# A two-lane decoder kernel: weights prepared later, the second lane begun at once, row maxima sent in blocks of eight heads

## The chip, the cores and the metric

One core of one Trainium2 chip runs the whole program. The metric is the device time of one execution in microseconds, the median of several runs. Smaller is better.

## The reference

Two decoder layers in float32 on x of shape (4, 256, 128). Layer 0 is self-attention of 16 heads of 8 columns with a learned relative bias that is added after the softmax, cross-attention to a context (16 heads of 64, a padding mask and a causal mask), and a feed-forward part whose activations and weights are quantized, with a depthwise convolution and SiLU. Layer 1 is causal self-attention with linear biases, a second attention over the heads of each token, and a mixture of eight experts with two chosen. Each part reads the layer norm of x and adds to x.

```
attn = softmax(einsum('bhqd,bhkd->bhqk', q, k) * scale)        # layer 0, first part
out  = einsum('bhqk,bhkd->bhqd', attn + rel_bias, v)           # 16 heads, 256 keys
...
scale = 1 / clip(mean(abs(w)), 1e-5); wq = clip(round(w*scale), -1, 1) / scale
```

The quantized weights need the mean absolute value of each weight matrix, and cross-attention needs, for rows whose keys are all closed, the product Wv Wo; both are found once, on the chip, before they are used.

## The kernel before

The batches are shared out to two lanes, A (batches 0 and 1) and B (batches 2 and 3). Each lane has its own half of the free on-chip memory, four of the eight PSUM banks, and its own program of six stages: `rel_attention` (tiles named l0a), `cross_attention` (l0x), `quantized_ffn`, `alibi_attention` (l1a), `head_attention` (l1x) and `expert_ffn` (moe). Each engine has one queue and works in its order. That order is written out by hand as text in `TURNS` (L2389 on): "A4 W1 A5" means four steps of lane A, one of the weight program W, five of lane A. A step is what a stage's program does between two `yield`s. The times behind `yield` order the parts within a stage; between the lanes only `TURNS` counts. Nothing is reordered at run time: a step that waits for a semaphore holds all behind it on its engine. L in SyncE's turns is the loading of weights that reuse the place of earlier ones: first the weights of l1x (when both lanes have left l0a), then the experts' (when both have left l0x).

**W**, `weight_levels` (L2129), loads most weights, converts constants to bfloat16, and prepares the quantized weights and the product Wv Wo: a sum of absolute values (DVE, L2174), a matmul with ones (L2198), five DVE operations to the levels (L2179 to L2192), eight transposes of Wv (L2201), two copies by ACT (L2213), sixteen matmul records for the product (L2206) and a scaled copy (L2217). Its buffers lie at the start of lane B's memory and it writes to lane B's banks 0 to 3. So lane B's first stage waits for it (`ready(..., "arena")`, L2259, on the semaphore `levels`), and in `TURNS` lane B's first TensorE step stands behind 32 steps of lane A.

**The first stage, l0a.** It normalizes x, transposes it (L172) and the context (L639), and for each of four token tiles projects q, k and v (L653), splits q and k into bfloat16 parts (DVE L572 and L575; POOL L493 and L496), stacks them (POOL L502, ACT L537), transposes the stacks (L668) and copies them out to `qkT` (DVE L465, ACT L517). Before that POOL clears the buffers (L483 to L488).

**The attention loop** is the class `Attention`, used by l0a and l1a. A softmax without overflow needs each row's maximum before the exponentials. So every head is multiplied twice: `tensor_S` makes the scores row by row and `vector_max` (L330) takes the negated maxima. When all 16 heads of a batch are done, `vector_parts` (L332) splits the maxima into three bfloat16 parts by four or five small chained DVE operations, `tensor_shift` (L238) transposes them, `vector_shiftT` (L356) copies them, and `sync_shift` (L251) sends them by DMA into three spare rows of the query tile. `tensor_E` then makes the transposed scores with the maxima already taken off, ACT exponentiates (L364), and `tensor_PV` multiplies with the values (L292). A score job is one head in l0a and one to four heads in l1a (`self.jobs`): 16 jobs a batch in l0a, 12 in l1a. Batch 0's jobs all run before the loop, in l0a as pairs of heads whose 64-row matmuls alternate between the two halves of the array (`tensor_S_pair`, L296, two PSUM banks); batch 1's are spread over the first twelve heads of the loop (`ahead`, one bank, L226). After the first shift TensorE also runs eight matmuls whose result nobody reads (L248). In l0a, a fourth of the stack copies are ACT's (`by_scalar`, L428).

## Time and profile before

| | us |
|---|---|
| median of 3 runs | 611.25 |
| lowest and highest | 607.7, 611.59 |
| the profiled execution's own time | 614.77 |
| its span, first to last instruction | 613.0 |
| TensorE busy in it | 533.3 |
| DVE busy | 420.4 |
| mean granted TensorE clock | 0.948 |

The span is cut into stretches to read it: a stretch where TensorE is busy nearly all the time at a granted clock of 1.00 can't be shortened without taking matmuls away; a stretch where it idles, or where its clock is granted at half (0.50 in the profile: 1.2 instead of 2.4 GHz), holds the time that an order of work can win or lose. The mean clock of a stretch lies between the two.

### The profile page before, as it was taken

How to read it: one execution, taken by the hardware profiler on the slowest of the kernel's cores; microseconds unless marked ns; L12 is line 12 of the kernel's file. 1: busy time of each engine (PE TensorE's matmuls, PEld its weight loads, DVE VectorE, ACT ScalarE, POOL GpSimd, SP SyncE). 2: the span in 40 equal slices, each digit the busy share in tenths (PEclk: the TensorE clock that was granted, in tenths of full speed). 3: DMA queues.
4: the chain of work that ended last, by engine and by line, in shares of the span. 5: the costliest groups of instructions: out<-in, count | busy, mean ns of one | idle time of the engine just before them, and what ended most of it. 6: DMA issues, size and time to landing. Idle time of an engine off the chain costs nothing.

```text
span 613.0 us, 12971 instructions
## 1 busy us (share of the span) xinstructions
PE 533.3 (87%) x4858; PEld 328.1 (54%) x4858; DVE 420.4 (69%) x1229; ACT 328.5 (54%) x809; POOL 193.8 (32%) x288
## 2 busy tenths in 40 slices
PE   4767797998999989877995679988998989999995
PEld 2433344344555656556453556666666866755554
DVE  5784664574454774898769876757548677589796
ACT  2413444457767785597644346544675548364341
POOL 5553300042235454332621031001023221434765
PEclk9966889999999999889997799999999999999998
DMA  8700000000002000000237105210000000402101
GB/s 290 280 1 3 2 3 3 2 3 2 2 18 120 2 1 2 2 1 1 66 111 267 26 12 163 79 31 2 4 3 2 2 2 3 139 0 80 59 2 34
DMA packets 25816, 27.92 MB, mean 46 GB/s; under 512 B 18177, under 2 KB 22794, under 8 KB 24858
## 3 DMA queue, kind: packets, MB, share of 16 engines
q1 hardware_dynamic: 25754, 27.10, 13.3%
q8 instruction: 39, 0.64, 0.4%
q14 instruction: 23, 0.19, 0.1%
HBM read 22.14 MB, written 4.75 MB: 44 GB/s over the span
## 4 chain that ended last, share of the span: by engine, by line
PE 66%; DVE 17%; ACT 5%; issue 4%; DMA 2%; POOL 2%; SPq 2%; POOLq 0%; DVEq 0%; ACTq 0%
PE B_banks L2086 5%; PE A_banks L292 4%; PE A_banks L2086 4%; PE B_banks L292 3%; DVE A_l0a_nmax L330 3%; PE A_banks L1011 2%; PE A_banks L998 2%; PE B_banks L1852 1%; PE B_banks L2118 1%; PE B_banks L998 1%; PE A_banks L951 1%; PE A_banks L1852 1%; PE A_banks L953 1%; PE B_banks L953 1%; PE B_banks L1862 1%
## 5 line engine op out<-in xcount | busy, mean ns | idle before, releaser
L818 POOL TENSOR_TENSOR A_l0x_prob<-A_l0x_prob,A_l0x_inverted_sums 128x256 f32<-128x256 f32 (+1 forms) x32 | 25.9, 829 | 54.1 <-DVE A_l0x_inverted_sums L932 54.0
L818 POOL TENSOR_TENSOR B_l0x_prob<-B_l0x_prob,B_l0x_inverted_sums 128x256 f32<-128x256 f32 (+1 forms) x32 | 27.1, 866 | 41.1 <-DVE B_l0x_inverted_sums L932 41.1
L2086 PE MATMUL A_banks<-A_moe_xT,w_moe_rows 128*128 128x512 f32 x72 | 35.1, 600 | 0.0
L330 DVE TENSOR_REDUCE B_l0a_nmax<-B_banks 128x2 f32<-128x512 f32 x32 | 21.5, 688 | 19.3 <-PE B_banks L226 13.6
L2086 PE MATMUL B_banks<-B_moe_xT,w_moe_rows 128*128 128x512 f32 x72 | 34.5, 596 | 0.0
L364 ACT ACTIVATE A_l0a_expT<-A_banks 128x512 f32<-128x512 f32 x32 | 18.3, 598 | 26.9 <-PE A_banks L316 26.9
L835 ACT ACTIVATE B_l0x_prob<-B_l0x_prob,B_l0x_nmax 128x128 f32<-128x128 f32 x64 | 28.3, 444 | 6.2 <-DVE B_l0x_nmax L914 6.2
L330 DVE TENSOR_REDUCE A_l0a_nmax<-A_banks 128x2 f32<-128x512 f32 x32 | 21.4, 689 | 13.8 <-PE A_banks L226 12.0
L835 ACT ACTIVATE A_l0x_prob<-A_l0x_prob,A_l0x_nmax 128x128 f32<-128x128 f32 x64 | 28.2, 446 | 2.2 <-DVE A_l0x_nmax L914 2.2
L364 ACT ACTIVATE B_l0a_expT<-B_banks 128x512 f32<-128x512 f32 x32 | 18.6, 599 | 11.6 <-PE B_banks L316 11.5
L998 PE MATMUL B_banks<-w_const_rows,B_l0x_prob 128*128 128x128 f32 x96 | 17.4, 292 | 7.9 <-ACT B_l0x_probT L852 5.0
L914 DVE CUSTOM_DVE_ANT_0 A_l0x_prob<-A_banks,A_l0x_mask_q 128x128 f32<-128x128 f32 x64 | 19.0, 353 | 7.2 <-PE A_banks L986 6.0
L1982 ACT ACTIVATE B_moe_h<-B_banks,w_moe_rest_rows 128x512 f32<-128x512 f32 x18 | 12.3, 684 | 20.3 <-PE B_banks L2086 20.3
L1715 POOL TENSOR_TENSOR A_l1x_prob<-A_l1x_prob,A_l1x_rz 128x512 f32<-128x512 f32 x8 | 8.3, 1042 | 46.2 <-DVE A_l1x_rz L1796 46.2
L852 ACT ACTIVATE B_l0x_probT<-B_banks 128x384 f32<-128x384 f32 x32 | 15.5, 484 | 13.5 <-PE B_banks L998 13.5
L364 ACT ACTIVATE A_l1a_expT<-A_banks 128x384 f32<-128x384 f32 x32 | 14.9, 494 | 13.9 <-PE A_banks L272 13.9
L364 ACT ACTIVATE B_l1a_expT<-B_banks 128x384 f32<-128x384 f32 x32 | 15.3, 494 | 11.7 <-PE B_banks L272 11.5
L852 ACT ACTIVATE A_l0x_probT<-A_banks 128x384 f32<-128x384 f32 x32 | 15.6, 488 | 11.0 <-PE A_banks L998 11.0
L330 DVE TENSOR_REDUCE B_l1a_nmax<-B_banks 128x2 f32<-128x512 f32 (+1 forms) x24 | 16.1, 686 | 6.1 <-PE B_banks L234 6.0
L914 DVE CUSTOM_DVE_ANT_0 B_l0x_prob<-B_banks,B_l0x_mask_q 128x128 f32<-128x128 f32 x64 | 18.9, 349 | 1.1 <-PE B_banks L986 0.9
L998 PEld LDWEIGHTS B_banks<-w_const_rows,B_l0x_prob 128*128 128x128 f32 x96 | 10.9, 146 | 15.9 <-issue 8.8
L2086 PEld LDWEIGHTS A_banks<-A_moe_xT,w_moe_rows 128*128 128x128 f32 x72 | 12.7, 190 | 11.9 <-issue 10.8
(612 smaller groups left out, 1574.5 us busy)
## 6 DMA issues: line engine op xcount, KB each, us to landing
w_toeplitz_rows<-in_toeplitz_rows SPq DMA_DIRECT2D x1, 3072.0 KB, 15.7
w_moe_rows<-in_moe_rows SPq DMA_DIRECT2D x1, 2304.0 KB, 8.6
w_l1x_rows<-in_l1x_rows SPq DMA_DIRECT2D x1, 2048.0 KB, 8.6
A_l1x_values<-A_l1a_v_tokens SPq DMA_DIRECT2D x4, 512.0 KB, 2.6
A_l1x_v_groups<-A_l1x_values SPq DMA_DIRECT2D x16, 128.0 KB, 3.2
B_l1x_values<-B_l1a_v_tokens SPq DMA_DIRECT2D x4, 512.0 KB, 3.2
B_l1x_v_groups<-B_l1x_values SPq DMA_DIRECT2D x16, 128.0 KB, 3.2
w_l0x_vo_rows<-in_l0x_vo_rows SPq DMA_DIRECT2D x1, 1024.0 KB, 8.8
```

The costliest lines, as they stand in the source:

```text
L292: ins = pe.matmul(bank[r:r + self.rows, second:S], lhsT, rhs, start=(part == 0), stop=(part == parts - 1), skip_group_check=True)
L330: dve.tensor_reduce(out, scores, AX, ALU.max, negate=True).then_inc(self.s_mx.sem, 1)
L364: act.activation(self.expT[:, u % self.ring, :], self.exp_bank(u)[:, 0:self.W], ACT.Exp, scale=self.scale).then_inc(self.s_p.sem, 1)
L818: ins = pool.tensor_tensor(pair, pair, bcast(rz[:, g % 2, i, :], 2, n), ALU.mult)
L835: ins = act.activation(part, part, ACT.Exp, bias=nmax[:, b, i, h:h + 1], scale=-1.0, accum_out=zsum[:, g % 2, i, u % 2:u % 2 + 1])
L852: act.activation(probT[:, u % 4, :], bank[2][:, 0:W], ACT.Copy).then_inc(s_pt.sem, 1)
L914: ins = dve.tensor_tensor_reduce(prob[:, (2 * p + j) % RING, at:at + n], bank[j][:, at:at + n], mask_q[:, b, at:at + n], 1.0, 3e38, ALU.ad ...
L953: ins = pe.matmul(bank[n % 3][:, :], w["l0x_k"][:, c * P:(c + 1) * P], cT[:], start=True, stop=True)
L998: ins = pe.transpose(bank[2][:, c * P:(c + 1) * P], prob[:, u % RING, c * P:(c + 1) * P], w["ident"][:])
L1011: ins = pe.matmul(bank[3][HD * j:HD * (j + 1), part * P:S], vals[:, b * SB + part, h * HD:(h + 1) * HD], pT[:, S:W] if part else pT[:, 0:S ...
L1982: act.activation(h1[:, n % 2, :], hidden_bank(2 * n)[:, :], ACT.Identity, bias=w["moe_b1"][:, e, part:part + 1]).then_inc(s_h1.sem, 1)
L2086: pe.matmul(hidden_bank(k)[:, :], w["moe_w3" if which else "moe_w1"][:, ORDER[i], part, :], xT[:], start=True, stop=True).then_inc(s_h.sem, 1)
```

## The change

Four edits come together.

1. `weight_levels` becomes part of lane A's side: its buffers lie at the end of lane A's memory, its matmuls use lane A's bank 0 only, in four rounds (sum, four transposes, four transposes, product), and it waits until lane A has copied out its last shift (`bank_left`). Its turns stand in the middle of lane A's attention loop. The uses of `levels` wait in l0x instead of in lane B's l0a. The loads of the table `toeplitz` and of the l0x weights go ahead of its raw weights.
2. Lane B begins with the others: its first TensorE turn stands behind 4 steps of lane A. Each lane's POOL clears its buffers before the norm, and the context is transposed after x (bank 3).
3. The maxima go in blocks of `HB` = 8 heads, four blocks a stage instead of two; 12 heads' jobs (`AHEAD`) run before the loop and the others are spread over the whole loop. The first shift stands between job 8 and job 9. The paired form of the score jobs and the eight matmuls without a reader go. Stack copies of the last two tiles are all ACT's.
4. All of `TURNS` is new. SyncE's second late load stands behind one SyncE step of lane A's l1a instead of behind six.

```diff
-EARLY = 4
+HB = 8
+AHEAD = 12
...
+    def due(self, n):
+        return min(self.BLOCKS * self.JOBS, -(-(n + 1 + AHEAD) * self.JOBS // HB))
+    def completed(self, n):
+        k = self.due(n) // self.JOBS
+        return k - 1 if n >= 0 and k * self.JOBS > self.due(n - 1) else None
     def score_bank(self, m):
-        return self.bank[m % 2 if m < self.JOBS else 0]
+        return self.bank[m % 2 if m < self.JOBS else (m + 1) % 2 if m < self.first else 0]
...
-        if b == 0:
-            for _ in range(8):
-                pe.matmul(self.bank[2][:, :], self.w["ident_bf"][:], self.w["other_token"][:]..., start=True, ...)
+        self.shifted = k
...
-    by_scalar = [n % 4 == 3 for n in range(STEPS)]
+    by_scalar = [n % 4 == 3 or n >= 4 * SB for n in range(STEPS)]
...
     def gpsimd(pool):                                  # l0a
-        yield 2.0
+        yield 0.0
+        pool.memset(vals[:], 0.0).then_inc(s_init.sem, 1)
         pool.memset(stack[:, :, 0, :, 6 * HD:SW], 0.0)
...
-        for u in range(a.JOBS):                        # l0a and l1a, on TensorE
+        for u in range(a.first):
-            if u % 2 == 0:
-                a.tensor_S_pair(pe, u)
+            if u == a.JOBS:
+                a.tensor_shift(pe, 0)
+            a.tensor_S(pe, u)
...
         for n in range(U + 8):
-            if h == H - EARLY and b + 1 < NB:
-                a.tensor_shift(pe, b + 1)
+            k = a.completed(n - 1)
+            if k is not None:
+                a.tensor_shift(pe, k)
...
+    st.at = lane.end - 3 * P * 4 - (2 * HID * 2 + HP * P + 16) * 4       # weight_levels(lanes[0], ...)
-        for group in ("const_16", "l0a", "B_x"):
+        for group in ("const_16", "l0a", "B_x", "toeplitz", "padding", "l0x_vo", "l0x"):
     def tensor(pe):
-        yield 9.5
+        yield 60.0
+        pe.wait_ge(*lane.bank_left)
         pe.wait_ge(*s_part(1))
         pe.matmul(bank[0][:, 0:2], w["ones"][:], part[:], ...).then_inc(s_sum.sem, 1)
+        for i in range(2):
+            pe.wait_ge(*(s_vT(1) if i else s_mean(1)))
+            for c in range(4):
+                ins = pe.transpose(bank[0][:, c * P:(c + 1) * P], w["l0x_v"][:, ...], w["ident"][:])
+        pe.wait_ge(*s_vT(2))
...
 TURNS = {
     "tensor":
-        "A4 W1 A5 W1 A23 B1 A3 B1 A3 B2 A4 B2 ...
+        "A4 B2 A2 B2 A5 B2 A3 B3 A4 B2 A1 B3 A10 B3 ... A1 B1 A2 W2 B2 A1 B1 W1 A2 B1 W1 ...
     "gpsimd":
-        "A15 B2 A1 B14 A11 ...
+        "A2 B1 A1 B1 A3 B1 A3 B3 A2 B2 ...
     "sync":
-        "W2 A1 W11 B1 A2 B2 L1 A6 L1 A3 B5 ...
+        "W1 A1 W1 B1 W11 A1 B1 A1 B1 A2 B2 L1 A1 L1 A7 B3 ...
```

## Rows read from the trace of the kernel before

**Rows 1.** The page: its first line and the busy time of each engine.
```profile
span 613.0 us, 12971 instructions
...
PE 533.3 (87%) x4858; PEld 328.1 (54%) x4858; DVE 420.4 (69%) x1229; ACT 328.5 (54%) x809; POOL 193.8 (32%) x288
```

**Rows 2.** Busy time by stretch: us, width, five engines' busy us, PEclk granted clock, DMA.
```profile
0.00:31.00 31.00, 17.62 (x106) 11.37 (x106) 20.09 (x59) 10.51 (x29) 16.61 (x34) 0.98 0.77 282
...
31.00:48.00 17.00, 10.55 (x56) 5.28 (x58) 12.83 (x26) 3.48 (x9) 10.16 (x16) 0.73 0.01 2
...
48.00:99.00 51.00, 42.67 (x408) 20.25 (x407) 31.48 (x76) 23.04 (x54) 8.08 (x19) 0.80 0.01 2
...
99.00:120.00 21.00, 18.89 (x159) 8.27 (x160) 11.53 (x31) 10.14 (x21) 1.02 (x1) 0.92 0.01 2
...
120.00:170.00 50.00, 47.96 (x420) 22.29 (x420) 26.23 (x109) 33.00 (x89) 14.31 (x20) 1.00 0.01 2
...
240.00:290.00 50.00, 41.27 (x336) 30.53 (x335) 41.07 (x151) 32.94 (x95) 16.79 (x23) 0.93 0.01 1
...
290.00:340.00 50.00, 39.77 (x269) 23.80 (x268) 39.10 (x119) 26.47 (x76) 15.78 (x43) 0.90 0.46 144
...
340.00:360.00 20.00, 14.59 (x123) 11.60 (x121) 16.52 (x48) 7.21 (x11) 0.01 (x1) 0.81 0.01 2
```

**Rows 3.** The chain that ended last, two pieces of it: start us, us, what.
```profile
97.10 2.21 DMA B_l0a_qkT<-B_l0a_shiftT
...
167.68 1.86 PE B_banks L292 x32
```

**Rows 4.** Timeline, 4 to 48 us: start us, us, engine, line, operation.
```profile
7.32 1.47 DVE L164 TENSOR_SCALAR A_l0a_xn<-A_x,A_l0a_mv,A_l0a_rstd 128x128 f32<-128x128 f32 x4
...
22.69 0.86 DVE L148 BATCH_NORM_STATS2 B_l0a_bn<-B_x 128x6 f32<-128x128 f32 x4
...
35.67 3.88 DVE L164 TENSOR_SCALAR B_l0a_xn<-B_x,B_l0a_mv,B_l0a_rstd 128x128 f32<-128x128 f32 x4
...
36.21 2.69 POOL L486 MEMSET B_l0a_vals<- 128x3072 f32 x1
...
47.91 0.39 PE L316 MATMUL A_banks<-A_l0a_qkT 64*128 64x256 bf16 x4 [1.83 <-DMA A_l0a_qkT<-A_l0a_shiftT]
```

**Rows 5.** Timeline of TensorE: the score matmuls of lane A and the shift.
```profile
27.95 0.39 PE L302 MATMUL A_banks<-A_l0a_qkT 64*128 64x256 bf16 x4 [1.05 <-DVE A_l0a_nmax L330]
...
44.07 0.28 PE L244 MATMUL A_banks<-w_ident_bf,A_l0a_parts 128*128 128x128 bf16 x2
...
44.19 1.89 PE L248 MATMUL A_banks<-w_other_token,w_ident_bf 128*128 128x512 bf16 x8
...
48.14 0.38 PE L226 MATMUL A_banks<-A_l0a_qkT 64*128 64x256 bf16 x2
```

**Rows 6.** Groups by line, 0 to 110 us: busy us, mean ns of one, idle before.
```profile
L330 DVE TENSOR_REDUCE A_l0a_nmax<-A_banks 128x2 f32<-128x512 f32 x32 | 21.4, 689 | 13.8 <-PE A_banks L226 12.0 <-PE A_banks L302 1.8
...
L502 POOL COPY A_l0a_expT<-A_l0a_split 128x256 bf16<-128x256 bf16 (+1 forms) x16 | 5.6, 393 | 0.3
...
L712 PE MATMUL A_banks<-w_const_rows,A_l0a_xT 128*128 128x128 f32 x16 | 3.4, 297 | 1.3 <-ACT A_l0a_xT L555 1.3
...
L496 POOL TENSOR_TENSOR A_l0a_split<-A_l0a_rest_qk,A_l0a_split 128x256 bf16<-128x256 f32 x4 | 2.7, 669 | 0.3
...
L2206 PE MATMUL B_banks<-w_l0x_vo_rows,B_wq_vT 128*128 128x128 f32 x16 | 2.0, 276 | 0.0
...
L345 DVE CAST A_l0a_parts<-A_l0a_nmax 128x32 bf16<-128x32 f32 x2 | 0.4, 182 | 0.1
```

**Rows 7.** Busy time by a short stretch, columns as in the second group.
```profile
52.00:54.00 2.00, 2.00 (x5) 0.59 (x4) 1.02 (x2) 0.67 (x2) 0.00 (x0) 0.50 0.00 0
```

**Rows 8.** Timeline of lane A's second attention, at its first shift.
```profile
349.85 0.28 PE L244 MATMUL A_banks<-w_ident_bf,A_l1a_parts 128*128 128x128 bf16 x2 [3.65 <-DVE A_l1a_parts L354]
```

**Rows 9.** Timeline of SyncE's queue: the load of the experts' weights.
```profile
322.74 0.57 SPq L2249 DMA_DIRECT2D w_moe_rows<-in_moe_rows  x1
```

More of the change, by code:

```diff
@@ L216, in tensor_S @@
     def tensor_S(self, pe, m):
-        b, at = divmod(m, self.JOBS)
-        c, h, n = self.jobs[at]
+        b, c, h, n = self.job(m)
         bank = self.score_bank(m)
-        if b:
+        if m == self.JOBS or m >= self.first:
             pe.wait_ge(*self.s_mx(m))
@@ L364, in scalar_exp @@
         act.activation(self.expT[:, u % self.ring, :], self.exp_bank(u)[:, 0:self.W], ACT.Exp, scale=self.scale).then_inc(self.s_p.sem, 1)
-def ahead(n, jobs):
-    b, h = divmod(n, H)
-    if b + 1 >= NB:
-        return range(0)
-    done, now = (min(jobs, k * jobs // (H - EARLY)) for k in (h, h + 1))
-    return range(jobs * (b + 1) + done, jobs * (b + 1) + now)
 def split_columns(part_of):
@@ L677, in tensor @@
                     transpose_stack(n)
-        for u in range(a.JOBS):
+        for u in range(a.first):
             yield SCORES + 1.2 * u - 0.4
@@ L1593, in tensor @@
             ins.then_inc(s_stT.sem, 1)
-        for u in range(a.JOBS):
+        for u in range(a.first):
             yield SCORES + 3.0 + 0.75 * u - 0.4
@@ L2155, in sync @@
             sp.dma_start(raw[:, i, :], raw_dram[i]).then_inc(s_raw.sem, 16)
-        for group in ("l0x_vo", "toeplitz", "padding", "l0x", "l1a", "ffn", "l1x_rest", "moe_rest"):
+        for group in ("l1a", "ffn", "l1x_rest", "moe_rest"):
             yield
@@ L2160, in vector @@
     def vector(dve):
-        link = Chain(dve, lane)
+        link = Chain(dve, st)
         yield 3.9
```

284 lines of the change are left out of this document (144 added, 140 removed), and 46 rows, old and new, of the table TURNS.

## Prediction

> **What bounds the kernel now.** I read the page first: TensorE is busy 533 of 613 us [rows 1], so it is the bound on the average, and what an order can win is the rest: 80 us of idle time, and time at half clock. Then the table of busy time by stretch shows where these lie [rows 2]. I multiply TensorE's busy time by the mean granted clock, which gives its work in us at full clock (an estimate, since a mean is used): 0 to 31 us: 17.62 x 0.98 = 17.3. 31 to 48: 10.55 x 0.73 = 7.7. 48 to 99: 42.67 x 0.80 = 34.1. 99 to 120: 18.89 x 0.92 = 17.4. 120 to 170: 48.0. So the first 120 us do only 76.5 us of work and leave 43.5, while from 120 on TensorE is nearly full at clock 1.00, a rate of 0.96. The second hole is 240 to 360: 120 - 41.27 - 39.77 - 14.59 = 24.4 us idle, with clocks of 0.93, 0.90 and 0.81.
>
> Third, why the start is empty. Lane B's norm runs at 22.69, its normalized x is written only at 35.67 [rows 4], its first exponential scores come after the DMA of 97.10, and its last product of values is at 167.68 [rows 3]. Lane A's first exponential scores are at 47.91 and had waited 1.83 us for the shift's DMA [rows 4]. Until 48 the rate is 25.0/48 = 0.52, with lane A going from TensorE to DVE and back alone: a pair of score jobs, then 1.05 us of waiting for the maxima [rows 5].
>
> **Part 1, lane B at once.** Total work to the state that before has at 170: 17.3 + 7.7 + 34.1 + 17.4 + 48.0 = 124.5 us. The change alters it so. A pair of heads takes 0.39 us for four matmuls, a single job 0.38 for two [rows 5]: before, a lane has 8 pairs and 16 singles, 3.1 + 6.1 = 9.2; after, 32 singles, 12.2. That is +3.0 a lane, +6.0. Two more shifts a lane at 0.28 [rows 5]: +1.1. The eight matmuls without a reader go, 1.89 a lane [rows 5]: -3.8. W's matmuls move, they aren't added. Sum 127.8.
>
> When do both loops begin? By 48 TensorE has done 25.0; without W (about 4; its product alone is 2.0 [rows 6]), the readerless 1.9 and some 3 of lane B, lane A's preparation is some 16, and with 12 single jobs (4.6) for 8 pairs (3.1) it is 17.6. Two lanes: 35, of which I put 33 before the loops. POOL bounds the pace: it needs 0.67 + 5.6/4 = 2.1 us a token tile for two of its three steps [rows 6], so eight tiles take at least 17 us, after both lanes' clearing (the longest fill is 2.69 [rows 4]) and norms. DVE has 24 maxima of 0.689 [rows 6], 16.5 us, beside the splits. I take 45 us (bounds 41 and 49: lane A alone needed 48 with 16 maxima before the loop in place of 12, and there is more beside it).
>
> Left are 127.8 - 33 = 95 us of work. The two loops are: per lane eight groups of values at 1.86 [rows 3], 16 pairs of exponential scores at 0.39 [rows 4], 20 jobs at 0.38, transposes 3.4 [rows 6]: 14.9 + 6.2 + 7.6 + 3.4 = 32.1, both 64.2. The other 31 are projections, which before ran at 0.96: 32 us. At what rate two loops run together is the open cost. Its bounds are 34.1/51 = 0.67 (48 to 99, one loop beside a preparation) and 0.96. I take 17.4/21 = 0.83, from 99 to 120, the one stretch in which, for most of it, both loops run [rows 2]. That gives 64.2/0.83 = 77 us. W now lies inside: TensorE waits behind its sum for DVE, and twice for ACT's copies, 0.5 us or so each; I take 2 us (0 to 4). Sum: 45 + 32 + 77 + 2 = 156, against 170: -14 us. With the bounds of the rate: 146 (-24) and 175 (+5).
>
> Clearing buffers is moved too. While POOL filled lane B's values from 36.21 for 2.69 us, DVE's four normalizing operations took 3.88 us; lane A's took 1.47 at 7.32, beside shorter fills [rows 4]. After the change POOL goes from lane A's norm straight to lane B's long fill, so lane A's may take 3.88: +2.4 us (0 to 2.4), inside the 41 to 49.
>
> The Trainium skill says on this (SBUF — State Buffer, "Who interferes with whom") that VectorE in a two-port mode and GpSimd lock each other out for a whole instruction; by it every one of lane A's four could meet a fill. Lane B's row agrees with such a lock and lane A's is milder, and by the page the start would be some 4 us later instead of 2.4.
>
> **Part 2, blocks of eight heads.** In the loop a stage now sends three shifts, not one. Each costs DVE four or five operations near 0.18 [rows 6] and a copy, about 1.1 us; over four stages 8 more, 9 us of DVE, whose busy time is 420 us of 613 [rows 1]. Each is finished four heads before it is needed, so the chain of DVE, TensorE, DVE and DMA (4 x 0.18, 0.28, a copy of about as long, 2.21 [rows 3, 5, 6]: 3.5 us) is covered; without that cover it would cost 3.5 us a block. The first shift is covered by the four jobs after it: that is inside the 45. In l1a lane A's TensorE stood 3.65 us before its first shift [rows 8], in a stretch of clock 0.81 [rows 2]. Nine jobs stand there instead of twelve, and three of them behind the shift. I take -3 us for lane A (bounds -5 and +1, since DVE is busy 16.52 of 20 us there and gets the extra operations), and nothing for lane B, whose l1a runs beside work of lane A.
>
> **Part 3, the rest of the turns.** From 170 on I cost them at +3 (bounds -3 and +8): the lag of lane B behind lane A, in steps, is smaller than before (lane B is at 43 to 61% when lane A is at 50 to 66%, against 37 to 51%), and with less lag both lanes sit in the feed-forward part or in the maxima of l1a together. There the cover, the other lane's projections, is thinner. SyncE now loads the experts' weights after one step of lane A's l1a instead of six [rows 9]; it waits for lane B's end of l0x. As long as that end comes before lane A's l1a it costs nothing.
>
> **Sum.** -14 - 3 + 3 = -14 on the profiled 614.77 us, 600.8. That execution lies 3.5 us above the median of the runs, 611.25, so the forecast is 597.
>
> **Rival 1, the loops overlap fully** (rate 0.96, l1a -5, rest 0): -24 - 5 = -29, 582. For: two lanes always have something else to issue. Against: in 99 to 120 they did not. 0.16.
>
> **Rival 2, the time comes back later.** The start gains 10 to 14, but between 240 and 360 DVE is the limit (41.07, 39.10 and 16.52 busy [rows 2]), the lanes meet there and lose 8, and the second late load holds lane A's DMAs: -4 or so, 607. Or the clearing and POOL's tiles hold lane B so that it doesn't really begin early; the same size. 0.2.
>
> **Rival 3, slower.** The place is the double loop of l0a. TensorE's queue is in order, a score job waits for its lane's DVE maximum, and the other lane's work stands behind it; the gaps let the clock fall. This happened before: at 52 to 54 TensorE was busy all of 2.00 us at clock 0.50 [rows 7], 6 us after the eight readerless matmuls. If the double loop runs like 48 to 99, at 0.67, the 170 becomes 175; with +2.4 for the fills, -1 for l1a and +6 for the lost lag the sum is +12: 623. It decides from a rate of 64.2/(170 - 79) = 0.71 downwards. 0.1.
>
> The Trainium skill (TensorE: Matmul & The Clock Gate, "HAM oscillation — how this bites in real kernels") warns of this too: waits between bursts of matmuls let the engine fall back to half rate. The row at 0.50 agrees. By it, taking the readerless matmuls out would leave the clock lower and the third rival would be likelier.
>
> **Chances and range.** Main case 0.54 (own range 590 to 604), rivals 0.16, 0.2, 0.1. A measurement of this kernel tells about 1%, 6 us, from no change. Faster by over 1% (below 605): 0.54 + 0.16 + a fifth of rival 2 = 0.74; within 1%: 0.15; slower: 0.11. The range 583 to 612 leaves out half of rival 1 and rival 3.
>
> **What would show it.** Right: lane B's first projection near 18 us instead of past 39.5 (35.67 + 3.88); both lanes' first exponential scores between 41 and 49; lane B's last product of values near 150 instead of 168; TensorE's work by clock of 64 us or so in the double loop at a rate near 0.83; no wait of TensorE on a shift's DMA over 0.5 us; lane A's wait before its first shift in l1a below 1 us; W's steps between lane A's last shift and its last exponentials with waits of 2 us together. Wrong: granted clocks below 0.8 between 45 and 110; waits for maxima in the double loop of over 15 us; more idle time of TensorE between 240 and 360 than 24 us; a SyncE queue that stands on the late load while lane A's l1a needs it.

## The result and the profile after

The changed kernel takes 603.0 us (median of 4 runs, 600.85 to 606.53) beside 610.0 for the kernel before on the same chip (4 runs, 607.7 to 611.59): ratio 0.990, 95% interval 0.987 to 0.993. That is 1.0% faster, 7.0 us, where 14 us (2.3%) were forecast. The profiled execution took 606.53 us against 614.77 before, 8.2 us less; each lies at or above the slowest of the four executions of its kernel. Two executions among the runs below, 1653 and 2665 us long, were disturbed and are left out.

The page of the changed kernel, its first line and the busy time of each engine; they answer to [rows 1]:

```profile
span 604.6 us, 13037 instructions
...
PE 522.7 (86%) x4832; PEld 323.9 (54%) x4842; DVE 427.1 (71%) x1261; ACT 330.7 (55%) x819; POOL 191.4 (32%) x288
```

TensorE is busy 10.6 us less and the span is 8.4 us shorter: its idle time did not fall, its busy time did. The busy time by stretch of the changed kernel, in the columns of [rows 2]:

```profile
0.00:31.00 31.00, 15.54 (x104) 9.53 (x104) 21.19 (x59) 12.13 (x36) 24.36 (x49) 1.00 0.78 281
31.00:48.00 17.00, 14.60 (x103) 6.79 (x102) 14.67 (x28) 12.21 (x30) 8.67 (x19) 0.72 0.01 3
48.00:99.00 51.00, 41.47 (x407) 19.19 (x408) 33.05 (x87) 21.45 (x46) 0.00 (x0) 0.79 0.01 2
99.00:120.00 21.00, 20.18 (x239) 10.80 (x239) 11.10 (x39) 12.04 (x27) 0.00 (x0) 1.00 0.01 3
120.00:170.00 50.00, 49.30 (x320) 22.31 (x318) 25.86 (x115) 32.74 (x92) 16.33 (x22) 1.00 0.00 1
240.00:290.00 50.00, 38.04 (x292) 27.36 (x292) 40.94 (x146) 34.15 (x102) 17.32 (x25) 0.91 0.01 1
290.00:340.00 50.00, 39.61 (x263) 24.16 (x260) 41.61 (x125) 23.78 (x56) 14.66 (x47) 0.92 0.47 141
340.00:360.00 20.00, 18.23 (x124) 10.45 (x125) 15.86 (x41) 9.74 (x29) 4.43 (x17) 0.91 0.32 97
```

The reader is to compare three rows. 48 to 99, which was to be the double loop at a rate of 0.83, reads 41.47 us at a clock of 0.79 and stood at 42.67 at 0.80 before: TensorE is no fuller there. 31 to 48 is fuller (14.60 busy for 10.55), but at a clock of 0.72. And 0 to 31 is emptier. Only 99 to 170 is visibly fuller (1.5 us idle for 4.2, clock 1.00 throughout). How full a stretch is doesn't say how far the two lanes have come in it; that is read below.

A finer sum shows it in three parts: over windows of 2 us, idle is the width less TensorE's busy time, work is busy time by granted clock, and loss is the rest of the busy time, what the half clock costs. I use these words below; the sums are good to a few us, no better, for two reasons. Neighbouring records overlap: busy time falls by 10.6 us, but the busy times of all groups of matmul records, added up, by only 6.1. And a trace is one execution: in 240 to 360, where the score jobs of l0a have no part, the kernel before loses 10.0 us to the half clock, and with nothing but l0a's score jobs changed 5.4.

| us | before: idle, work, loss | after: idle, work, loss |
|---|---|---|
| 0 to 48 | 19.8, 24.5, 3.6 | 17.9, 25.7, 4.5 |
| 48 to 100 | 8.7, 34.4, 8.9 | 9.5, 33.5, 9.0 |
| 100 to 170 | 3.8, 64.7, 1.5 | 1.5, 68.5, 0.0 |
| 170 to the end | 47.4, 384.8, 10.8 | 52.9, 369.7, 12.0 |

By 170 us the changed kernel has done 127.7 us of work, just what the forecast said was needed for the state that before has at 170 (127.8). But it had come further than that state. Lane B's last values, its first projection of l0x and a matmul of lane A's l0x, in the changed kernel and then the last two in the kernel before:

```profile
149.31 1.05 PE L312 MATMUL B_banks<-w_toeplitz_rows,B_l0a_vals 128*32 128x256 f32 x16
152.38 1.02 PE L960 MATMUL B_banks<-w_l0x_vo_rows,B_ctxT 128*128 128x512 f32 x2
...
173.51 0.66 PE L982 MATMUL A_banks<-w_l0x_vo,A_l0x_ctx_sum_by_token 128*128 128x128 f32 x4
```

```profile
170.32 1.02 PE L951 MATMUL B_banks<-w_l0x_vo_rows,B_ctxT 128*128 128x512 f32 x2
...
177.28 0.66 PE L973 MATMUL A_banks<-w_l0x_vo,A_l0x_ctx_sum_by_token 128*128 128x128 f32 x4
```

Lane B is 18 to 19 us ahead of its old time (its last values end at 150.4; before, the group at 167.68 [rows 3] ends at 169.5) and lane A 4. From the end of its l0a to 170 lane B does 9.0 us of work that the kernel before does only after 170 (the changed kernel's instructions on lane B's banks alone):

```profile
150.40:170.00 19.60, 9.03 (x18) 1.00 0.00 0
```

Lane A does 1.8 us more in the same way (167.5 to 170). Take these off, and the state that before has at 170 took 117 us of work and was reached near 160. So the start gained some 10 us of the 14 forecast (an estimate, from the busy time on each lane's banks; taken at other states between 164 and 290 us it gives 8 to 11), and behind 170 next to nothing was added to it or lost: the span is 8.4 us shorter.

The start, from the timeline of the changed kernel (start us, us, engine, line, operation; in brackets the idle time before and what ended it):

```profile
6.73 2.66 POOL L482 MEMSET B_l0a_vals<- 128x3072 f32 x1
7.30 4.11 DVE L2179 CAST w_ident_bf<-w_const_rows 128x128 bf16<-128x128 f32 x1 [1.68 <-DMA w_const_rows<-in_const_rows]
7.44 4.04 DVE L2180 CAST w_mask_q<-w_const_rows 128x128 bf16<-128x128 f32 x1
...
12.29 1.10 DVE L165 TENSOR_SCALAR A_l0a_xn<-A_x,A_l0a_mv,A_l0a_rstd 128x128 f32<-128x128 f32 x4
...
12.77 1.16 PE L173 MATMUL A_banks<-w_const_rows,A_l0a_xn 128*128 128x128 f32 x4 [12.77 <-DVE A_l0a_xn L165]
...
17.98 1.61 DVE L165 TENSOR_SCALAR B_l0a_xn<-B_x,B_l0a_mv,B_l0a_rstd 128x128 f32<-128x128 f32 x4
...
20.76 1.53 PE L656 MATMUL B_banks<-w_l0a_rows,B_l0a_xT 128*128 128x384 f32 x4
```

Lane A's normalized x is written at 12.29, not at 7.32 [rows 4]: DVE first waits 1.68 us for the constants, and its first two casts to bfloat16 then stretch over 4 us. POOL clears lane B's buffers beside them, in fills of 2.66, 0.95, 0.79 and 0.38 us that end at 11.33; the casts end at 11.41 and 11.48. TensorE's first instruction of all is at 12.77. Lane B's first projection, 20.76, is near the forecast 18.

The exponential scores (line 327 now) of lane A and the first of lane B, same columns:

```profile
44.06 0.39 PE L327 MATMUL A_banks<-A_l0a_qkT 64*128 64x256 bf16 x1
...
49.00 0.61 PE L327 MATMUL A_banks<-A_l0a_qkT 64*128 64x256 bf16 x4
...
53.38 0.61 PE L327 MATMUL A_banks<-A_l0a_qkT 64*128 64x256 bf16 x4
...
59.73 0.39 PE L327 MATMUL A_banks<-A_l0a_qkT 64*128 64x256 bf16 x4
...
61.81 0.40 PE L327 MATMUL B_banks<-B_l0a_qkT 64*128 64x256 bf16 x4 [0.22 <-DVE B_l0a_nmax L340]
```

Lane A's first, at 44.06, lies in the 41 to 49 that was forecast for both; lane B's first is at 61.81. Lane A's pairs come 4 to 6 us apart. Four matmuls take 0.61 us there and 0.39 outside: that is the half clock. The two stretches around it, in the columns of [rows 2]:

```profile
44.00:62.00 18.00, 14.22 (x104) 5.92 (x104) 11.77 (x27) 7.11 (x14) 0.00 (x0) 0.58 0.01 2
62.00:80.00 18.00, 14.57 (x132) 6.23 (x132) 10.80 (x29) 6.58 (x13) 0.00 (x0) 0.72 0.01 2
```

In 2 us windows that is 8.0 us of work in the first 18 us and 9.8 in the next, 0.44 and 0.54 of full rate; in the kernel before 9.1 and 11.3. From 80 to 100 the changed kernel does 17.7 in 20, from 100 to 116 15.2 in 16: the double loop is not slow once the clock is full. TensorE's four longest sums of waits in 31 to 120 (what waited, for what: us in total, times, longest):

```profile
PE A_banks L248 <- DVE A_l0a_nmax L340: 4.6, 8, 0.9
PE B_banks L248 <- DVE B_l0a_nmax L340: 2.3, 3, 0.9
PE A_banks L264 <- DVE A_l0a_parts L367: 1.6, 1, 1.6
PE B_banks L248 <- DVE B_l0a_shiftT L373: 1.0, 1, 1.0
```

The idle gaps are short, 1.6 us at the longest, and the half clock around them costs more than they do: 11.0 us of loss against 7.2 of idle time in 44 to 80. No shift's DMA is among the waits, as forecast, and lane B's last values at 149.3 are where the forecast had them (near 150).

### The profile page after: what moved, and what is told of

It is laid out like the page before. It is cut to its first block, busy times and chain, and to the rows that moved or that the text cites. A ratio compares the mean times of both kernels' runs of the same rounds, so it can differ in the third digit from the quotient of the medians.

```text
span 604.6 us, 13037 instructions
## 1 busy us (share of the span) xinstructions
PE 522.7 (86%) x4832; PEld 323.9 (54%) x4842; DVE 427.1 (71%) x1261; ACT 330.7 (55%) x819; POOL 191.4 (32%) x288
## 4 chain that ended last, share of the span: by engine, by line
PE 64%; DVE 19%; ACT 5%; issue 5%; POOL 3%; DMA 2%; SPq 1%; POOLq 0%; DVEq 0%; ACTq 0%; another core or an unknown queue 0%
PE A_banks L312 4%; PE B_banks L312 4%; PE A_banks L2098 3%; PE B_banks L2098 3%; PE A_banks L1020 2%; PE A_banks L1007 2%; DVE A_l0a_nmax L340 2%; PE B_banks L1007 2%; PE B_banks L1823 2%; PE B_banks L1020 2%; PE B_banks L248 1%; PE B_banks L975 1%; PE A_banks L975 1%; PE B_banks L962 1%; PE B_banks L960 1%
## 5 line engine op out<-in xcount | busy, mean ns | idle before, releaser
L379 ACT ACTIVATE A_l0a_expT<-A_banks 128x512 f32<-128x512 f32 x32 | 18.6, 608 | 29.5 <-PE A_banks L327 29.5
L160 POOL TENSOR_TENSOR A_l0a_rstd<-A_l0a_ve,w_const_rows 128x4 f32<-128x4 f32 x2 | 2.0, 1012 | 79.9 <-DVE A_l0a_ve L156 79.9
L379 ACT ACTIVATE B_l0a_expT<-B_banks 128x512 f32<-128x512 f32 x32 | 18.5, 606 | 10.2 <-PE B_banks L327 10.2
L1007 PE MATMUL B_banks<-w_const_rows,B_l0x_prob 128*128 128x128 f32 x96 | 17.7, 295 | 6.4 <-ACT B_l0x_probT L859 4.1
L1994 ACT ACTIVATE A_moe_h<-A_banks,w_moe_rest_rows 128x512 f32<-128x512 f32 x18 | 12.3, 684 | 18.5 <-PE A_banks L2098 18.5
L859 ACT ACTIVATE A_l0x_probT<-A_banks 128x384 f32<-128x384 f32 x32 | 15.5, 484 | 10.9 <-PE A_banks L1007 10.8
L340 DVE TENSOR_REDUCE A_l1a_nmax<-A_banks 128x2 f32<-128x512 f32 (+1 forms) x24 | 16.3, 689 | 5.9 <-PE A_banks L256 5.6
```

The costliest lines, as they stand in the source:

```text
L340: dve.tensor_reduce(out, scores, AX, ALU.max, negate=True).then_inc(self.s_mx.sem, 1)
L379: act.activation(self.expT[:, u % self.ring, :], self.exp_bank(u)[:, 0:self.W], ACT.Exp, scale=self.scale).then_inc(self.s_p.sem, 1)
L859: act.activation(probT[:, u % 4, :], bank[2][:, 0:W], ACT.Copy).then_inc(s_pt.sem, 1)
L1007: ins = pe.transpose(bank[2][:, c * P:(c + 1) * P], prob[:, u % RING, c * P:(c + 1) * P], w["ident"][:])
L1994: act.activation(h1[:, n % 2, :], hidden_bank(2 * n)[:, :], ACT.Identity, bias=w["moe_b1"][:, e, part:part + 1]).then_inc(s_h1.sem, 1)
```

## The experiments

All ran beside the kernel before (609.4 to 611.1 us in these sets). Ratios are to it, with their 95% interval; "against the changed kernel" is the ratio divided by 0.9899. Where the text says by how much the start was reached sooner or later, it is the state of both lanes that before has near 174 us, found as above.

### The matmuls without a reader

In the kernel before (line 245 on) they are taken out:

```diff
-        if b == 0:
-            for _ in range(8):
-                pe.matmul(self.bank[2][:, :], self.w["ident_bf"][:], self.w["other_token"][:]...)
```

> The kernel before with one edit: the eight matmuls without a reader after each first shift (L248) are gone, nothing else. Theory 1 (the change's gain is TensorE work taken away: between the two traces TensorE's idle time went from 79.7 to 81.9 us, its loss to the half clock from 24.9 to 25.5, its work from 508 to 497): removing them alone gives most of the gain, 4 to 7 us against before. Rival (the gain is from lane B's early start, and the readerless matmuls were hidden in the wait for the shift's DMA): 0 to 1.5 us, or slower, since the clock falls earlier.

Measured: 616.6 us, 1.009 [1.0059, 1.0122], 0.9% slower: the theory that the gain is TensorE work taken away fell. In the changed kernel the same eight go back, in l0a in front of the first exponential scores (behind the twelve score jobs), in l1a behind the first shift:

```diff
+    def readerless(self, pe):
+        for _ in range(8):
+            pe.matmul(self.bank[2][:, :], self.w["ident_bf"][:], self.w["other_token"][:]..., ...)
...
         wait_copied(pe, STEPS - 1)                     # l0a
+        a.readerless(pe)
...
             if u == a.JOBS:                            # l1a
                 a.tensor_shift(pe, 0)
+                a.readerless(pe)
```

> The changed kernel with the eight readerless matmuls put back, once per stage, before the first exponential scores in l0a and after the first shift in l1a. Theory 1: the gain over before shrinks from 7 us to 0 to 3 us. Rival (they cost nothing, or they keep the clock up in the double loop of l0a, which ran at a clock of about 0.67 from 48 to 80 us): the same as the changed kernel within 1 us, or faster.

Measured: 605.8 us, 0.9933 [0.9913, 0.9952]. So taking them out costs the kernel before 5.5 us and gives the changed kernel some 2, by the ratios; the second is at the edge of what the intervals tell. Put another way: with them in both kernels the rest of the change is worth 4 us, with them in neither some 12. The stretch 44 to 62, first of the kernel before without them, then of the changed kernel with them (the changed kernel's own stands above):

```profile
44.00:62.00 18.00, 12.72 (x63) 5.81 (x60) 9.74 (x22) 6.91 (x18) 4.52 (x12) 0.59 0.01 2
```

```profile
44.00:62.00 18.00, 14.95 (x102) 6.04 (x100) 10.63 (x25) 6.43 (x13) 0.00 (x0) 0.69 0.01 2
```

With them the clock is 0.69 in the changed kernel, without them 0.58; in the kernel before 0.68 and 0.59. The clock is higher with them in both. The clock is not all of it: without them the kernel before has 7.7 us less work, 9.8 us more idle time and 0.4 us more loss over its span (2.2 more up to 100 us). But before, they fill a wait for a DMA in which there is nothing else; in the changed kernel other work of both lanes stands behind them. That this is why they cost there is the reading that fits; no run varied it by itself. They are 8.4 us of records in all, l1a's as well as l0a's, and the sum had counted only l0a's 3.8.

### Score jobs in pairs or one by one

The changed kernel gets the paired form back for the jobs ahead of the loop:

```diff
-            a.tensor_S(pe, u)
+            if u % 2 == 0:
+                a.tensor_S_pair(pe, u)
```

> The changed kernel with the 12 score jobs before l0a's loop issued as six pairs again (four matmuls on both halves of the array), all else as in the change. The prediction's term: +6 us of TensorE work for both lanes from single jobs, of which 12 of 32 jobs are undone here, so 2 to 2.5 us less work. Theory A (the term was real and on the path): 1.5 to 2.5 us faster. Rival (single jobs of one lane run beside the other lane's on the other half of the array, or DVE's maxima pace this stretch): 0, or slower by up to 2 us, since a pair waits for both maxima before it.

Measured: 609.3 us, 0.9988 [0.9973, 1.0003], 0.9% above the changed kernel. Its stretch 44 to 62:

```profile
44.00:62.00 18.00, 11.42 (x79) 4.98 (x81) 12.41 (x27) 7.00 (x13) 0.00 (x0) 0.50 0.01 2
```

A clock of 0.50 throughout. A pair waits for the maxima of both banks, and the queue stands meanwhile for the other lane too; in 44 to 80 the idle time is 11.0 us for 7.2, and the longest sum of waits is a new one, of lane B's pairs:

```profile
PE B_banks L325 <- DVE B_l0a_nmax L354: 3.9, 3, 1.7
```

The start is reached 5.6 us later. Both expectations had missed: one had it faster, the other slower by 2 us at most. The reverse in the kernel before, with its own turns:

```diff
-            if u % 2 == 0:
-                a.tensor_S_pair(pe, u)
-            else:
+            a.tensor_S(pe, u)
+            if u % 2:
                 yield
                 transpose_stack(4 * SB + u // 2)
```

> The kernel before with its first sixteen score jobs issued one head at a time and each waiting for the maximum that frees its own bank, instead of in pairs that wait for both maxima; the turns are those of before. The reverse test (pairs in the changed kernel) had cost 6 us. Theory (the single jobs help where two lanes share TensorE, and cost more work of it where one lane runs alone; in the kernel before each lane's sixteen first jobs run alone): 0 to 2 us faster, ratio 0.997 to 1.000. Rival (single jobs are worth 6 us wherever they stand, and the early lane B is worth nothing): 0.988 to 0.992. Other rival (the weight loads, which a pair shares out better, cost 3 us more per lane): 1.003 to 1.010.

Measured: 608.2 us, 0.9963 [0.9937, 0.9989]: 2.3 us faster, just past what the theory gave. So a third of the change's 1% is to be had by this edit alone. And the change with pairs kept ahead of l0a's loop is worth nothing that can be measured: in these turns, which were made for single jobs, the early lane B pays only together with them.

### A later fill, and lane B late again

Lane B's POOL waits with its clearing until lane A's normalized x is written, and lane A's norm is let go ahead of it:

```diff
     def gpsimd(pool):
+        w[f"{lane.name}_xn"] = s_xn(TT)
         yield 0.0
+        if lane.name == "B":
+            pool.wait_ge(*w["A_xn"])
```

> The changed kernel with one wait more on POOL: lane B's buffers are cleared only once lane A's normalized x is written. In the changed kernel DVE's two casts of the constants took 4.11 us beside POOL's fill of 2.66 us, and lane A's transposed x came at 12.77 us instead of 7.86. Theory 2 (the start is bound by lane A's chain through DVE, POOL and TensorE): lane A's transposes begin near 8.5 to 9 us and the whole is 2 to 4 us faster than the changed kernel. Rival (POOL's and DVE's total work bounds the start, so lane B loses what lane A wins; or the double loop after it absorbs it): within 1 us of the changed kernel.

Measured: 602.5 us, 0.9884 [0.9862, 0.9907], not told from the changed kernel. The collision is gone, lane A's x is there 4.3 us earlier:

```profile
8.00 1.11 DVE L165 TENSOR_SCALAR A_l0a_xn<-A_x,A_l0a_mv,A_l0a_rstd 128x128 f32<-128x128 f32 x4
...
9.17 2.66 POOL L485 MEMSET B_l0a_vals<- 128x3072 f32 x1 [2.26 <-DVE A_l0a_xn L165]
...
42.79 0.39 PE L327 MATMUL A_banks<-A_l0a_qkT 64*128 64x256 bf16 x1
```

but its first exponential scores come only 1.3 us earlier. The fill is not the cause of the missing gain.

The other way round, `TURNS` with lane B's steps of l0a later, which gives it a third to a half of its old lag back: its first TensorE step stands behind 19 steps of lane A (before 32, changed kernel 4), its 60th behind 96 (before 118, changed kernel 85), the other engines' strings to match.

```diff
 TURNS = {
     "tensor":
-        "A4 B2 A2 B2 A5 B2 A3 B3 A4 B2 A1 B3 A10 B3 ...
+        "A19 B2 A4 B1 A2 B1 A9 B2 A1 B3 A7 B1 A1 B2 ...
```

> The changed kernel with another order: all of lane B's steps of l0a are put 25 us later at the start, fading to none at 170 us; lane A, the weight steps, the blocks of eight heads and everything after 170 us are as in the change. Theory S (lane B's early start is worth something only if the rest of the order uses it; here it does): slower than the changed kernel by 10 us or more, with lane B's stages late by 10 us or more at every later milestone. Rival (lane B's start is worth nothing, since TensorE's total work decides): within 4 us of the changed kernel.

Measured: 632.5 us, 1.038 [1.0357, 1.0408], 4.9% above the changed kernel. Lane A's l0a then ends at 139.6 (changed 124.1, before 119.1), and the start is reached 24 us later. It was the expected direction, 10 us or more. But it is 3.8% slower than the kernel before, which has all of the lag. So the merged order is bad here, and what an early lane B is worth by itself is not shown by this run: these turns were made by a rule and not tuned, and other orders cost as much (below).

### The pace of the maxima

`vector_max` reads fewer keys, so that the shift isn't the reference's; everything else stays. Half of the keys, in either kernel:

```diff
-            out, scores = self.nmax[:, b, :, h], bank[:, :].rearrange("p (c k) -> p c k", c=SB)
+            out, scores = self.nmax[:, b, :, h], bank[:, :].rearrange("p (c k) -> p c k", c=SB)[:, :, 0:P]
```

> The changed kernel with each maximum of l0a taken over the first 128 of the 256 keys only: the reduction reads half as much, so its 0.689 us become some 0.42, and TensorE's work is the same. The shift is then not the row's maximum (that part of the computation is changed). Theory D (from 28 to 110 us both lanes wait for DVE: TensorE to DVE and back is what paces l0a): 64 maxima by 0.27 us are 17 us of DVE, and 5 to 10 us of the whole go. Rival (the half clock and the in-order queue pace it): under 2 us.

> The kernel before with the same edit (maxima of l0a over half the keys). In it lane A's l0a runs alone on DVE until 35 us. Theory D: it gains as well, 3 to 8 us, since 12.0 us of DVE's idle time and 5.1 + 3.9 us of TensorE's lie between score jobs and maxima of lane A. Rival: under 2 us.

> The changed kernel with the maxima of lane-wide score jobs taken over half of the keys, as in an earlier run (0.978 of the kernel before) whose profiled execution was disturbed; sent for a profile. If the maxima hold back lane B's first exponential in the changed kernel, it starts before 56 instead of at 61.8, and idle time plus half-clock loss in 48 to 100 falls from 18.5 to under 13; if the order of turns and the half clock hold it, it starts after 59 and that sum stays over 16. Ratio 0.975 to 0.982.

An eighth of them (`0:32`):

> The changed kernel with these maxima over 32 of the 256 keys (the shift is then not the reference's). Theory (the maxima's round trips between TensorE and VectorE keep TensorE partly idle and thereby at half clock in 48 to 100 us): another 3 to 6 us beyond the half maxima, ratio to the kernel before 0.968 to 0.974, lane B's first exponential before 54. Rival (below half a maximum it is TensorE's own order and clock that bound the stretch): no further gain, 0.976 to 0.981.

> The kernel before with the maxima of lane-wide score jobs over 32 of the 256 keys, the pair of the run of the changed kernel with the same (ratio 0.9718). If the full maxima are what kept the change's gain from coming (the double loop of two lanes needs twice as many of them in its time), the kernel before gains less from this than the changed kernel: ratio 0.984 to 0.990, and the change is then worth 9 to 11 us between the two. If both gain alike, the change's worth stays at 6 to 7 us and the maxima's pace is a cost of both kernels, which the forecast only put in the wrong place: ratio 0.980 to 0.984. With half maxima the two had stood at 602.4 and 597 to 599.5 us, so the second is held more likely.

| a maximum takes | before | changed | changed to before |
|---|---|---|---|
| 0.69 us | 1 | 0.9899 [0.9872, 0.9926] | 0.990 |
| 0.42 us | 0.9882 [0.9856, 0.9907] | 0.9784 [0.9752, 0.9815] and 0.9822 [0.975, 0.9894] | 0.990 and 0.994 |
| 0.22 us | 0.9746 [0.972, 0.9771] | 0.9718 [0.9656, 0.978] | 0.997 |

The stretches 44 to 62 and 62 to 80, first the changed kernel, then the kernel before, both with an eighth:

```profile
44.00:62.00 18.00, 15.63 (x144) 6.91 (x144) 6.51 (x36) 9.59 (x19) 0.00 (x0) 0.67 0.01 3
62.00:80.00 18.00, 16.50 (x202) 7.94 (x196) 6.77 (x37) 9.02 (x20) 0.00 (x0) 0.91 0.01 2
```

```profile
44.00:62.00 18.00, 15.69 (x167) 7.72 (x165) 7.95 (x30) 10.77 (x30) 8.48 (x23) 1.00 0.01 3
62.00:80.00 18.00, 14.78 (x180) 7.77 (x177) 7.75 (x33) 8.56 (x21) 2.25 (x5) 0.91 0.01 3
```

In the changed kernel 0.47 us off a maximum brings 11 us, and the 127.7 us of work are done at 160 instead of 170: the round trips over DVE do hold this stretch, and 0.82 of full rate in 48 to 100, the forecast's 0.83, is what it would do with maxima that cheap. Lane B's first exponential scores came at 57.6 (60.3 with half maxima), still not at 45, and not before 54 as expected. But the kernel before gains 15 us from the same, more than either range that had been written down for it. Half-clock loss over its whole span goes from 24.9 to 16.0 to 9.1 us; the changed kernel's from 25.5 to 22.4 to 18.5 (one execution each). With half of the keys idle time and loss of the changed kernel in 48 to 100 fall from 18.5 to 12.2 us, as expected if the maxima hold the stretch, while lane B's first exponential scores stay behind 59, as expected if the order of turns holds them. So the run of the changed kernel alone would have misled: the maxima are a cost of both kernels, and they did not eat this change's gain. By the medians it would be smaller without them, 0.997; the intervals just leave room for the same 0.990.

### Filling for the clock

One matmul without a reader, 512 columns, in front of each pair of exponential scores in l0a's loop:

```diff
+        pe.matmul(self.exp_bank(u)[:, :], self.w["ident_bf"][:], self.w["other_token"][:]..., start=True, ...)
```

> The changed kernel with one more matmul without a reader (512 columns, bfloat16) before every pair of exponential scores in l0a's loop: 32 of them, 0.21 us each at full clock, 6.9 us more work. In the changed kernel TensorE loses 9.0 us to the half clock between 48 and 100 us. Theory C (the half clock in the double loop costs that much, and a busier queue avoids it): the loss falls to 3 us or less and the whole is the same as the changed kernel or up to 3 us faster. Rival (the clock falls anyway, or the work costs as much as it saves): 3 to 7 us slower than the changed kernel.

Measured: 612.5 us, 1.0054 [1.0028, 1.008], 1.6% above the changed kernel and past both ranges expected. Work rises by 9.7 us; loss in 48 to 100 falls only from 9.0 to 6.8. More filling did not pay in this stretch, where the other lane has work waiting.

### What W costs at its new place

The changed kernel and the kernel before without three quarters of W's eight transposes and seven eighths of its product (the lines of the changed kernel):

```diff
-            for c in range(4):
+            for c in range(1):
...
-        for c in range(HP):
+        for c in range(1):
```

> The changed kernel, which leaves out three quarters of the eight transposes that prepare W and seven eighths of its product (the output's W part is then not the reference's). Theory (W was hidden in idle time of lane A's start before, and now stands at 93 to 100 us in a stretch where TensorE is busy to 99%, so all that it takes there is paid; the profile of the changed kernel has 0.63 and 0.66 us of transposes, 2.00 us of product and 0.54 us of waits there): 2.5 to 4 us faster than the changed kernel, ratio to it 0.993 to 0.996, and the last value product of lane A about 3 us earlier than 115.8. Rival (W fills gaps there too, since the other lane's work can't go faster than its VectorE maxima): within 1 us of the changed kernel.

> The kernel before with the same part of W left out. Theory (its place at 14 to 22 us, while TensorE waits for lane A's first projections, hides it): 0 to 1 us against the kernel before, ratio 0.998 to 1.000. Rival (its casts and its place in front of lane A's projections delay the start): 2 to 3 us faster, ratio 0.995 to 0.997.

> The changed kernel without three quarters of W's transposes and seven eighths of its product, as in an earlier run (0.9896, with an interval of 0.5% to either side and a disturbed profiled execution), for a narrower interval and a profile. W paid in full: 2.5 to 4 us under the changed kernel, ratio 0.983 to 0.986. W hidden at its new place too: 0.988 to 0.991; the profile then shows lane A's last value product 0 to 1 us earlier than 115.8, with the gap filled by idle time or a lower clock.

Measured: 604.9 us, 0.9896 [0.9849, 0.9943]; 611.5 us, 1.0032 [1.0003, 1.006]; and again, for a narrower interval, 602.7 us, 0.9882 [0.9849, 0.9915]. In the kernel before it makes nothing faster, 0.3% slower if anything. In the changed kernel it changes nothing that can be measured either (0.17% less by the better run, give or take 0.4), though TensorE is busy 6.55 of 7.00 us at 93 to 100 (94%, not the 99% that the expectation had) and all the time from 94 to 101. W's steps of the changed kernel:

```profile
93.29 0.35 PE L2213 MATMUL A_banks<-A_wq_part,w_const_rows 128*128 128x2 f32 x2
93.99 0.63 PE L2219 MATMUL A_banks<-w_const_rows,w_l0x_vo_rows 128*128 128x128 f32 x4 [0.34 <-DVE w_ffn_wmean L2193]
95.31 0.66 PE L2219 MATMUL A_banks<-w_const_rows,w_l0x_vo_rows 128*128 128x128 f32 x4
98.20 2.00 PE L2224 MATMUL A_banks<-w_l0x_vo_rows,A_wq_vT 128*128 128x128 f32 x16
```

Busy time by stretch of the changed kernel without them, in 80 to 99:

```profile
80.00:99.00 19.00, 16.47 (x190) 8.01 (x182) 12.66 (x36) 8.83 (x20) 0.00 (x0) 0.91 0.01 2
```

The changed kernel has 16.68 us there at 1.00. Its variants with the later fill, the readerless matmuls, the fillers or cheaper maxima have a clock of 1.00 there, too, the one with pairs 0.91. So the room seems to go to clock, but there is one trace only without this part of W. Lane A's l0a ends at 124.2 for 124.1: by this, more than by the times, the theory of a paid W fell.

### Another order

Orders of turns searched off the chip, by a rough model of queues and waits with durations from the traces, for the changed kernel with the later fill and for the kernel before. Only `TURNS` differs.

```diff
-        "A4 B2 A2 B2 A5 B2 A3 B3 A4 B2 A1 B3 A10 B3 A3 B1 ...
+        "A4 B3 A3 B1 A5 B2 A2 B3 A7 B1 A2 B1 A6 B3 A4 B2 ...
```

> The changed kernel with the fill of lane A's normalized tokens let go first (as in the earlier run with lane B's fills later, 602.5 us), and with another order of turns, searched for that kernel: every turn of the five strings that merge lane A's, lane B's and W's steps may have moved, the steps themselves are the same. Theory (the loss is in how the two lanes' score jobs, shifts and value products are interleaved at 44 to 120 us, and the turns are the lever): at least 5 us faster than the changed kernel, ratio to the kernel before 0.965 to 0.980, lane B's first exponential before 58. Rival (the double loop is paced by maxima and by the half clock, whatever the order): 0.983 to 0.992, no better than the changed kernel. Other rival (an order searched off the chip meets waits that it did not foresee): above 1.00.

> The kernel before with another order of turns alone, searched in the same way; nothing else differs from the kernel before, so lane B's x is still normalized late and the score jobs are still in pairs. Theory (part of what the change brought is the new turns, not the early lane B): 3 to 10 us faster than the kernel before, ratio 0.984 to 0.995. Rival (the order of before is as good as its parts allow): 0.998 to 1.01.

Measured: 639.1 us, 1.0467 [1.0423, 1.0511], and 631.1 us, 1.0307 [1.0253, 1.036]. Both missed badly. The first one's lane B reaches its exponentials at 78.6, and 48 to 100 loses 14.2 us to the half clock; the model had no clock that falls in short waits. They show how much hangs on the turns, 3.1% against the kernel before and 5.7% against the changed one, and with that how little two kernels with different turns say of their other differences. No kernel here beats the changed one with all of the computation in it; the later fill equals it.

## Why the forecast was half right

The direction and the place were right: the gain is in the start, and it is there by 170 us. The size was not, 7 us for 14; on the profiled executions 8.4 of span, some 10 of them in the start.

**The failing step is the start of both loops, "I take 45 us (bounds 41 and 49)", with 33 us of work done by then.** At 45 TensorE had done some 24, and 31.7 at 61.8, when lane B's first exponential scores came. The work ahead of the loops was sized right; the time for it was 17 us short. What the step missed is a bound of its own: TensorE's first instruction is at 12.77, so 33 us by 45 asked for more than every microsecond there is at full clock. With lane A's transposes at 7.86, as before, there would have been 37, with little room for POOL's, DVE's and the half clock's share. The missing 17 us are made up so: the late x costs little (1.3 us of the 4.3 reached the first exponentials when it was put right), and 44 to 62 ran at 0.44, for which the eighth maxima bring 2.4 us of work and the readerless matmuls a clock of 0.69 for 0.58. Lane B's order in `TURNS` holds the rest, by elimination: with cheap maxima it still began at 57.6. That part wasn't shown by a run of its own.

**The work, 127.8 us, was the other miss, and it went the other way.** The state that before has at 170 took 117 us, 7 less than in the kernel before (123.6 in the same sums), where the forecast had 3.3 more. That is worth more than 10 us of time and hid most of the 17: near 160 was measured for 156 forecast, and this nearness is in part luck. Of the difference, single jobs are up to 6 us (below); the rest is not settled.

**The rate of 0.83 of the double loop** was right, where both loops ran. From 62 to 170 the kernel did 96.0 us of work in 108; the forecast had 95 in 109 (77 + 32). Stated as 48 to 100 it looks wrong, 0.64, because the loops didn't run together there. The row nearest to what stood there was 48 to 99 of before, which the forecast had as its lower bound and as the third rival's case.

**Single jobs +6.0:** in the records the score jobs of l0a take 7.6 us more (21.6 to 29.2). But a record also covers time in which another matmul runs beside it. In the sums of work the same edit adds 2.4 us to the kernel before (508.5 to 510.9), and the pairs put back ahead of the changed kernel's loop take 0.3 away. For the time the sign was wrong: single jobs make the kernel faster (0.9% in the changed kernel, 0.4% before), since each waits for one bank only.

**Where the 10 us of the start come from.** By 160 idle time and loss are 42.3 us, for 46.3 before by 170: 4 us. The other 7 are less work, 3.8 of them the readerless matmuls of l0a, which by the runs bring no time by themselves. Lane B's early steps fill 15 to 48 (idle 5.1 for 11.3), but 0 to 15 is 4.2 us emptier, since W's and the context's work went and the x is late; and in 48 to 100 idle time and loss stay what they were, 18.5 for 17.6. The kernel before already had lane B's preparation there. Two lanes in the same phase wait for the same DVE.

**Readerless matmuls:** -3.8 in the sum, 8.4 in the records; l1a's were overlooked. In time some -2 us, and only beside an early lane B.

**Fills +2.4:** lane A's normalizing took 1.10 us and not 3.88; the collision hit the two casts before it instead, and lane A's transposes began 4.9 us later than before (12.77 for 7.86). In time it costs about 0.5 us, inside the noise. The Trainium skill (SBUF — State Buffer, "Who interferes with whom") has VectorE in a two-port mode and GpSimd lock each other out for a whole instruction. The estimate of 4 us that the prediction made by it was near for the delay and wrong for the kernel's time. The casts of 4.11 and 4.04 us fit such a lock, but they outlast the one fill of 2.66 us beside which they start and end with the last of the fills.

**W +2:** 0. The waits were smaller than forecast too: one of 0.34 us, and 0.45 us of idle time in 93 to 100 altogether.

**l1a -3:** lane A's first shift there no longer waits (3.65 before, [rows 8]):

```profile
353.54 0.27 PE L264 MATMUL A_banks<-w_ident_bf,A_l1a_parts 128*128 128x128 bf16 x2
```

Idle time and loss of 240 to 360 go from 34.4 to 33.5 only. The wait went; whether the stretch gained by it can't be told, since two executions differ there by as much (31.6 in the kernel before with only l0a's score jobs changed).

**The rest +3:** behind 170 the forecast had 0 in all (-3 and +3). Measured are some 2 us lost of the 10 gained, though 4.6 us of l1a's readerless matmuls went, too. At the end of l1a lane B is 29.5 us ahead of its old time (434.0 for 463.5), lane A 3.3 behind (420.5 for 417.2). At the end they are 8.5 and 8.4 ahead. The lead moves from lane to lane; weighed by the work of both it stays at 6 to 12 us from 164 us to the end. Idle time and loss behind 170 rise from 58.2 to 64.9 us and work falls from 384.8 to 369.7: 10.8 of these 15.1 were done before 170, and 4.6 are l1a's readerless matmuls.

**The rivals.** None came as put. By the median, 7.0 us gained, the result lies between the main case (14) and rival 2 (4), nearer to the second. Rival 2 has the start gain 10 to 14 and the lanes lose 8 of it between 240 and 360; the start gained some 10, but nothing like 8 was lost there. Rival 3 had the right place, the half clock in the double loop, and a rate even under its 0.71 where it pointed; what it lacked is that this had been so before. In direction the clock gate's page (the Trainium skill, TensorE: Matmul & The Clock Gate, "HAM oscillation — how this bites in real kernels") agrees with the clocks of 0.58 and 0.69 without and with the readerless matmuls, though the waits in that stretch are 1.6 us and less; that they nevertheless cost time in the changed kernel only the run could say.

## What to carry to other kernels

Bound an early start by what the busiest engine can do until then: the time of its first instruction, plus the work, at the clock of the rows around it. A second stream of work beside the first fills the engine only where the first one leaves it with nothing to issue; if both go back and forth with the same second engine, the gaps stay, and the half clock around them. Read a gain by how far each stream has come, and not by how full the engine is up to some time: by work done up to 170 us this change seemed to have won nothing, and by the state of the lanes it had won all that it ever did. And when an experiment removes a suspected cost, remove it from the kernel before too: here it gave 11 us in the changed kernel and 15 in the other, which turned its meaning round.

## What was not expected of the hardware

Two casts of 128 by 128 took 4.11 and 4.04 us beside a row of fills on POOL that end when they do, and 0.23 and 0.22 with the fills put later, while four normalizing operations of the same size took 3.88 in one place [rows 4] and 1.10 to 1.95 in the others. Removing work from TensorE can go with a lower clock, so that no time is won: with most of W's matmuls gone from 93 to 100 us, the one trace of it has a clock of 0.91 in 80 to 99 for 1.00. Sixteen readerless matmuls less in each lane even cost the kernel before 5.5 us, though there the idle time rose by more than the loss. And cheaper maxima paid in great part through the clock: with an eighth of the keys the kernel before had 1.3 us less idle time (79.7 to 78.4) and 15.8 us less loss, the changed kernel 6.2 (81.9 to 75.7) and 7.0. These are single executions; the one of the kernel before has a mean clock of 0.948, where nearly all its others have 0.953 to 0.964, so a few us of the 15.8 are its own.
